# Layer normalisation in an attention and mixture-of-experts kernel: the normalising step moved from ScalarE to GpSimd

## What is computed

```python
def _layernorm(x, eps=1e-05):
    m = jnp.mean(x, axis=-1, keepdims=True)
    v = jnp.var(x, axis=-1, keepdims=True)
    return (x - m) / jnp.sqrt(v + eps)

x = x + xattn(_layernorm(x), ctx, ctx, w_proj, b_proj)
# xattn: softmax(q k^T / sqrt(16)) v per head, then @ w_proj.T + b_proj
x = x + ffn(_layernorm(x), Wg, W1, W2, W3)
# ffn: top 2 of 8 gate logits, softmax over the two;
# per expert silu(x W1) * (x W2), then W3; 682 hidden columns
```

## Time and profile before

| | |
|---|---|
| median of 3 runs | 885.32 us (885.25 to 887.26) |
| profiled execution | 882.82 us, span of its trace 881.0 us |
| busy: TensorE, VectorE | 786.4 us (89%), 602.0 us (68%) |
| busy: ScalarE, GpSimd | 557.1 us (63%), 439.7 us (50%) |
| granted TensorE clock, mean | 0.991 of full speed |
| DMA moved | 167.52 MB, mean 190 GB/s |

### The profile page before, as it was taken

The page is one execution under the profiler, slowest core; times in us unless marked ns, Lnnn a source line. Parts: engine busy times, 40 slices in busy tenths (PEclk is TensorE's granted clock), DMA queues, the critical chain, the costliest instruction groups (busy, mean ns, idle before and its releaser), DMA issues.

```text
span 881.0 us, 20060 instructions
## 1 busy us (share of the span) xinstructions
PE 786.4 (89%) x6472; PEld 481.1 (55%) x6472; DVE 602.0 (68%) x1224; ACT 557.1 (63%) x970; POOL 439.7 (50%) x431
## 2 busy tenths in 40 slices
PE   0578898989989898987989999997999999999995
PEld 0112233333333333322337788886888888888884
DVE  3888888989889898899725566553555555555553
ACT  3369789898898989867783544443444444444442
POOL 4565435787767778774634674223322222222222
PEclk9999999999999999999999999998999999999998
DMA  8585756867567685674184899999986688383832
GB/s 177 173 197 167 201 129 226 182 222 161 178 235 166 216 216 197 133 187 160 70 289 145 223 270 272 260 301 234 273 253 157 165 244 254 55 249 55 245 43 25
DMA packets 105955, 167.52 MB, mean 190 GB/s; under 512 B 54688, under 2 KB 83232, under 8 KB 101280
## 3 DMA queue, kind: packets, MB, share of 16 engines
q1 hardware_dynamic: 92448, 148.76, 58.9%
q0 software_dynamic: 13440, 17.90, 10.6%
HBM read 119.75 MB, written 42.55 MB: 184 GB/s over the span
## 4 chain that ended last, share of the span: by engine, by line
PE 39%; SPq 4%; issue 3%; ACT 3%; DMA 3%; POOL 2%; DVE 1%; POOLq 0%; ACTq 0%; DVEq 0%
PE ps L1371 8%; PE ps L1373 8%; PE ps L1375 8%; PE ps L1389 3%; PE ps L1393 3%; PE ps L1391 3%; PE ps L1294 2%; SPq L534 1%; ACT probs L839 1%; DMA slots<-fill 1%; DMA out<-y,aim 1%; POOL slots L472 1%; PE ps L1279 1%; PE ps L1398 1%; DMA w<-w_parts 1%
## 5 line engine op out<-in xcount | busy, mean ns | idle before, releaser
L970 DVE TENSOR_REDUCE neg_max<-ps 128x2 f16<-128x1024 f32 x256 | 309.2, 1221 | 35.5 <-PE ps L1266 31.0
L839 ACT ACTIVATE probs<-ps 128x1024 f32<-128x1024 f32 x256 | 259.0, 1024 | 59.4 <-PE ps L1279 58.9
L766 POOL DMA_INDIRECT out<-y,aim x72 | 113.4, 1575 | 247.6 <-DVE y L1197 174.9
L1371 PE MATMUL ps<-zt,w 128*128 128x256 f16 x792 | 216.9, 274 | 7.7 <-DMA w<-w_parts 5.8
L1373 PE MATMUL ps<-zt,w 128*128 128x256 f16 x792 | 216.7, 274 | 0.0
L1375 PE MATMUL ps<-zt,w 128*128 128x256 f16 x792 | 216.6, 274 | 0.0
L873 ACT ACTIVATE silu<-ps 128x256 f32<-128x256 f32 x216 | 82.6, 383 | 190.8 <-PE ps L1375 183.9
L1178 DVE SCALAR_TENSOR_TENSOR hid<-ps,silu 128x256 f32<-128x256 f32 x216 | 91.7, 425 | 134.4 <-ACT silu L873 130.2
L1294 PE MATMUL ps<-probs,v_ext 128*32 128x512 f32 x1024 | 138.1, 611 | 5.4 <-ACT heads L907 4.4
L1266 PE MATMUL ps<-k_stack,q_stack 48*128 48x512 f16 x512 | 104.1, 406 | 34.1 <-ACT probs L839 17.7
L1279 PE MATMUL ps<-q_stack,k_stack 49*128 49x512 f16 x512 | 101.7, 395 | 7.2 <-DVE neg_max L970 7.1
(11 more groups left out here) (126 smaller groups left out, 907.1 us busy)
## 6 DMA issues: line engine op xcount, KB each, us to landing
w<-w_parts SPq DMA_DIRECT2D x36, 1408.0 KB
w<-w_parts SPq DMA_DIRECT2D x36, 768.0 KB
w_in<-in_w SPq DMA_DIRECT2D x16, 704.0 KB, 5.2
v_ext<-in_v SPq DMA_DIRECT2D x8, 1024.0 KB, 5.4
k_stack<-k SPq DMA_DIRECT2D x48, 128.0 KB, 5.0
q_stack<-qt SPq DMA_DIRECT2D x48, 128.0 KB, 4.7
w_in<-in_w SPq DMA_DIRECT2D x8, 768.0 KB, 5.0
w_parts<-w_hi SPq DMA_DIRECT2D x16, 352.0 KB, 2.3
```

The source lines that it names most:

```text
L766: nc.gpsimd.indirect_dma_start(out=out, out_offset=bass.IndirectOffsetOnAxis(ap=aim[frm][:, t, 0:1].bitcast(U32), axis=0), in_=y[frm][:, t ...
L839: nc.scalar.activation(probs[g % 2][:, j:j + 2, k, :], pair_banks[PLACE["exp", u] % 3], ACT.Exp, scale=0.25).then_inc(s_exp, 1)
L970: nc.vector.tensor_reduce(neg_max[b % 2][:, i, c:c + 3:2], pair_banks[PLACE["max", u] % 3], AX.X, ALU.max, negate=True).then_inc(s_red, 1)
L1371: nc.tensor.matmul(dst, w[:, kk, 1, cols], z16[:, kk, :], start=(kk == 0), stop=False)
```

## The change

GpSimd normalises x and x2 itself, by tensor_scalar with two per-partition operands: (x + (−mean)) · rstd, four operations of 128 by 256 for each normalisation, 64 in all (L687 of the changed kernel). `shift` now holds the negated mean alone, so `inverse_root` has three operations, of which the negation doesn't wait for the root. ScalarE's 64 ACTIVATEs and their slots go. The other slot numbers are set anew.

```diff
-AT_CHOOSE = 44
-AT_CLEAR = -13
+AT_CHOOSE = 45
+AT_CLEAR = -15
-AT_K_IN = -22
-AT_K_LO = -4
+AT_K_IN = -20
+AT_K_LO = -8
-AT_PICK = 49
-AT_Q_HI = -13
-AT_Q_LO = -11
-AT_Q_PARTS = -4
-AT_SCATTER = 50
-AT_V_IN = 5
+AT_PICK = 50
+AT_Q_HI = -16
+AT_Q_LO = -12
+AT_Q_PARTS = -3
+AT_SCATTER = 51
+AT_V_IN = 4
-AT_W_LO = (3, 7, 14)
-AT_W_OUT = (1, 9, 13)
+AT_W_LO = (3, 7, 15)
+AT_W_OUT = (1, 8, 13)
-AT_X_IN = -27
-AT_X_NORM = (-14, -15, -16, -14)
+AT_X_IN = -28
-AT_X_ROOT = -14
+AT_X_ROOT = -16
-AT_Z_LO = 40
-AT_Z_NORM = (37, 37, 37, 37)
-AT_Z_ROOT = 36
-STEP_LN2 = (124, 138, 145, 146, 147)
-STEP_PREP = (-98, -96, -94, -92, -79)
+AT_Z_LO = 45
+AT_Z_ROOT = 37
+STEP_LN2 = (124, 138, 145, 144, 145)
+STEP_PREP = (-98, -94, -96, -90, -71)
...
-AT_ADD = (4, 8)
+AT_ADD = (7, 7)
...
-                pool.wait_ge(done, b * 4 + 1)
+                nc.gpsimd.tensor_scalar(sh[:, :], agg[:, :, 0], -1.0, None, ALU.mult).then_inc(done, 1)
+                pool.wait_ge(done, b * 3 + 2)
...
-                pool.wait_ge(done, b * 4 + 2)
-                nc.gpsimd.tensor_tensor(sh[:, :], agg[:, :, 0], rs[:, :], ALU.mult).then_inc(done, 1)
-                pool.wait_ge(done, b * 4 + 3)
-                nc.gpsimd.tensor_tensor(sh[:, :], sh[:, :], con[:, C_NEG:C_NEG + 1].to_broadcast([P, NT]),
-                                        ALU.mult).then_inc(done, 1)
+                pool.wait_ge(done, b * 3 + 3)
+
+            def normalise(to, x, rs, sh, done):
+
+                for i in range(NT):
+                    nc.gpsimd.tensor_scalar(to[:, i, :], x[:, i, :], sh[:, i:i + 1], rs[:, i:i + 1],
+                                            ALU.add, ALU.mult).then_inc(done, 1)
...
                     inverse_root(mv, rstd, shift, s_rstd, b)
+                    normalise(x_in, x_in, rstd, shift, s_qn)
...
                     inverse_root(mv2, rstd2, shift2, s_rstd2, b)
+                    ge(pool, s_zl, b)
+                    normalise(z_n, x2, rstd2, shift2, s_zn)
...
-                nc.scalar.activation(to[:, i, :], x[:, i, :], ACT.Identity, bias=sh[:, i:i + 1],
-                                     scale=rs[:, i:i + 1]).then_inc(done, 1)
```

More of the change, by code:

```diff
@@ L840, in exponentials @@
                                          scale=0.25).then_inc(s_exp, 1)
-            def normalise(to, x, rs, sh, i, done):
-                nc.scalar.activation(to[:, i, :], x[:, i, :], ACT.Identity, bias=sh[:, i:i + 1],
-                                     scale=rs[:, i:i + 1]).then_inc(done, 1)
             def misc(half_slot):
@@ L911, in _ @@
                     nc.scalar.copy(k16[0][:, :, :], kt_in[:, :, :]).then_inc(s_kh, 1)
[L912 to L919, removed]
                 for b in due(slot, AT_Q_HI):
```

## The result

The changed kernel takes 891.12 us (median of 10 runs, 888.04 to 893.75) against 885.00 in the runs of the kernel before beside it: a ratio of 1.0063 [1.0046, 1.0080], or 5.6 us slower. The forecast was 881.2; the range held the time, the sign was wrong.

The account below looks back on a forecast made before the run. The prediction took GpSimd's path plus 15.6 us of TensorE's program to close a 52.3 us ring. Its terms, −0.7 + 0.5 − 1.2 + 1.6 − 1.5 − 0.8 − 2.0 + 0, gave −4.1 from 885.32: 881.2 us, range 872.5 to 892.0.

Parts of the forecast that it names:

- The ring: Steady attention batches: GpSimd's path from one `choose` plus 15.6 us of TensorE's program to the next sets the 52.3 us period.
- (d): Four steady attention batches: period 49.1 + 8n = 52.7 against 52.3, +0.4 us each, +1.6 for four.
- n: Price of one new GpSimd normalising operation on 256 columns: taken as 0.45 us, from 0.36 up to 1.04.
- (a): Start of the kernel: GpSimd's root and four normalisations end at 10.93 instead of 12.29; −0.7 us (0 to −1.4).
- (g): z_n of batch 7, which TensorE waits 1.86 us for: no change, 0 (±1.9).
- The rival that priced them at 0.16: GpSimd's new operation: second operand costs as on the two-input row, n = 0.61; +1.0 us, 886.3; chance 0.20.
- (e): Last batch of attention: TensorE's wait for exponentials goes, −1.5 us, and half the clock drop behind it, −0.8.
- (c): Batch 2: `q_lo` now ahead of z's root, so TensorE's wait for it goes; −1.2 us (0 to −1.8).
- (b): Keys' load ahead of q_parts on SP's queue: first scores wait longer for q_stack; +0.5 us (0 to +3).
- (f): z_n of batch 6: TensorE's waits for z_n and `heads` behind ScalarE shrink; −2.0 us (0 to −3).
- The slower one: Rival: pointer form slow on GpSimd, z_n in the ring; decides from n = 0.66; at 1.04, 900.1 us; chance 0.20.
- The faster one: Rival: z_n doesn't bind, idle time in TensorE's 15.62 us absorbs it; period about 50.8, 873.6 us; chance 0.18.

Follow-up runs that it names:

- e1: The changed kernel with 12 more identity transposes on TensorE ahead of the first turn of z_n in batches 1 to 4: 886.0 us, ratio 1.0019.
- e3: The changed kernel with x's normalisation alone back on ScalarE, z staying on GpSimd: 878.85 us, ratio 0.9951 to the kernel before.
- e11: The changed kernel with constants 0 and 1 for x's two per-partition operands, so x is not normalised: 884.23 us in one execution.
- e12: e2 with z's root ahead of q_lo on GpSimd and ScalarE's four ACTIVATEs right behind the root: 892.04 us, ratio 1.0083 to the kernel before.
- e5: The changed kernel with the first turn of z_n half a slot later on TensorE: 880.93 us, ratio 0.9950 to the kernel before.
- e2: The changed kernel with z's normalisation alone back on ScalarE, x staying on GpSimd: 910.93 us, ratio 1.0311 to the kernel before.
- e4: The changed kernel with the load of the next keys back ahead of k_parts on SP's queue: 889.34 us, ratio 1.0051 to the kernel before.
- e9: e3 with the load of the next keys back ahead of k_parts: 876.19 us, ratio 0.9906 to the kernel before.
- e8: e3 and e5 together, with the load of the next keys back ahead of k_parts: 877.77 us, ratio 0.9914 to the kernel before.
- e10: e5 with x's root and normalisation back behind the pick, ahead of the scatter: 891.83 us, ratio 1.0072 to the kernel before.

## Why the prediction was wrong

**The ring was right (d).** Period 49.1 + 8n with 4n = 2.16 is 53.4; the windows at full clock are 53.25 and 53.55, e1's 53.3 to 53.6. z_n takes the place of the wait on `q_lo`, as forecast, and e3, e11 and e12 show x's operations in the ring. VectorE's wait of 1.17 + 0.24 is covered, as forecast: in the batch of 53.25 TensorE stands 0.52 and 0.75 for VectorE behind it and still 2.24 for z_n, so without the first two it would only stand longer for z_n.

**The price n was mis-sized.** "I take n = 0.45" came out as 0.54 in a row of four (2.16), 0.555 and 0.562 by the groups. Eight n in each of four batches make 32 × 0.09 = 2.9 us. ((a) and (g) hold 4n each as well, which the 32n of the prediction leaves out; that would be another 0.7.) I had left the per-partition operands at nothing because no row showed them; e11 measures 0.158 us for the two. The rival that priced them at 0.16 took 0.61, as its base from the long rows was 0.04 too high. The rule on small reads in the Trainium skill ("GPSIMD Engine Reference", section "Performance pitfalls for Q7 kernels") gave an estimated 0.17 us for two. e11's number is near it, though that section speaks of kernels that issue many small reads and doesn't say that an operand of tensor_scalar is one.

**The clock was counted on the wrong side.** The prediction had one term for it, a gain in (e), and none for the wait that it put on TensorE itself. Two short waits became one of 2.1 to 2.3 us in each steady batch, and in two of the four of the trace a spell at half clock followed. e1 prices this at 3.9 us. This, with n, turns −4.1 into +2.7, and is most of why the sign was wrong; with the 2.3 of (e) it is +5.0, of 5.6 measured.

**(e) failed.** Of −2.3 nothing came. The stage is 55.99 in e1 and 56.02 before. TensorE's wait of 1.49 for ScalarE's exponentials is gone, but the stage ends no sooner. VectorE is its fullest engine, busy 51.95 of the 56.02 before and 52.85 of the 55.99 in e1, and TensorE already waited for VectorE's maxima before the change, 1.52 and then 2.42:

```profile
398.62 0.39 PE L1279 MATMUL ps<-q_stack,k_stack 49*128 49x512 f16 x2 [2.42 <-DVE neg_max L970]
```

In the changed kernel's trace there are four such waits of 1.38 to 1.69 between 403 and 430 us, of which two:

```profile
403.26 0.40 PE L1270 MATMUL ps<-q_stack,k_stack 49*128 49x512 f16 x2 [1.60 <-DVE neg_max L961]
...
420.22 0.39 PE L1270 MATMUL ps<-q_stack,k_stack 49*128 49x512 f16 x2 [1.69 <-DVE neg_max L961]
```

The prediction took the wait for ScalarE as time gained and named no next-late engine there; that VectorE is that engine is read from these rows, no run changes its work. Nor did the spell go: the stage has one or two in the trace of every run. In the changed kernel's own trace it is 58.79, with two spells at half clock behind the two waits shown; e1, whose program is the same there, has a spell too and still 55.99, so 2.8 of the 9.3 between the two traces is no fixed cost.

**(a) to (c)** were −1.4 up to the first `choose`. It came 1.24 late in the changed kernel's trace, with the wait of 2.27 for q_stack and a spell, and 1.23 early in e1, whose program is the same up to there. In e1 the terms come out one by one: the first scores of batch 0 start at 23.95 against 24.66 before, 0.71 sooner ((a) had 0.7); those that wait in batch 1 at 69.05 against 69.32, so 0.44 of that is lost ((b) had 0.5); and from there to `choose` 0.96 is won ((c) had 1.2). One trace each is thin evidence for terms of this size: where the first scores of batch 0 start, runs with the same order up to there differ by 0.5 (23.70 in e5, 24.23 in e2). What (b) is worth in the changed kernel stays open: e4 doesn't tell it from nothing, and with x on ScalarE e9 and e8 put it at 4 and 3 us, past or at the far end of its bound.

**(f) and (g) held:** 48.89 to 47.07 is −1.82 (−2.0 forecast), 38.31 to 37.46 is −0.85 (0 ± 1.9). In (f) the wait for z_n is gone, and the one for `heads` is 1.20 in place of 1.75; in (g) the wait for z_n is 1.01 in place of 1.86. The experts didn't change, as said.

**The rivals.** The slower one had the place right (z_n in the ring) and the price too high: at n = 0.54 it would not have decided. What made the kernel slower was the clock on top, which none of the rivals held. The faster one fell in the changed kernel. With x off GpSimd's path e9 comes near to its time, 876.19 against 873.6, but not in its way: e9's spacings are 51.6 to 51.9, and TensorE still waits 1.14 to 1.41 for z_n. In e8, where it doesn't wait for z_n, they are 51.97 to 51.99, not the 50.8 of that rival.

## What to carry to other kernels

Work moved off a busy engine must be priced where it lands: if that engine's program closes a ring, each moved microsecond that no wait of that engine takes up is paid in every period, even for a result that is wanted much later, because all that stands behind it in program order comes later too. Here half of the move, z alone and the keys' load left where it was, is 0.9% faster than the kernel before, and the whole is 0.6% slower. When a step merges two short waits of TensorE into one, look at the granted clock behind it: here filling the wait with work of no use made the kernel 3.9 us faster.

## What the runs showed of the hardware

On GpSimd, a tensor_scalar of 128x256 in float32 takes 403 ns with two constants and 555 to 562 with two per-partition operands.

TensorE's granted clock fell to its lower level at waits of 2.25 and 2.26 us and not at 2.09 and 2.24; in e11 at waits of 2.00 and 2.25 and not at another of 2.25; in e12 at two of four waits of 1.42 to 1.43; in e10 at a wait of 1.24 and one of 1.27 some 2.6 us apart, and in e5 not at the one of 1.27 alone. A wait's length alone doesn't decide it in these runs. What decides it stays open. What a spell costs is plain from pairs of windows: 53.23 and 54.63 in e12, 1.4 us for one of 3.4; 53.4 and 55.80 in the changed kernel, 2.4 us for one of 6.8.
